# Ten of 32 weighted sums scaled on ScalarE and added on GpSimd, and three of eight stores issued one stage later

## What is computed

```python
def _L0_ffn_ref(x, router_w, router_b, expert_w, expert_b):
    xf = x.reshape(bs, h)
    S = softmax(xf @ router_w + router_b)            # 16 experts
    G, idx = top_k(S.T, bs // 16)                    # each expert takes 256 rows
    out = einsum('ekh,hd->ekd', xf[idx], expert_w) + expert_b
    return zeros.at[idx].add(G[..., None] * out)

x = x + 0.5 * _L0_ffn_ref(layernorm(x), ...)         # stage A
x = x + _L0_attn_ref(layernorm(x), ...)              # stage B: differential attention
x = x + 0.5 * _L0_ffn_ref(layernorm(x), ...)         # stage C
```

## Time and profile before

| | |
|---|---|
| time, median of 3 runs | 1705.95 us (1698.11, 1705.95, 1711.32) |
| the profiled execution's own time | 1705.67 us |
| its span, first to last instruction | 1703.3 us |
| busy: PE, DVE, ACT, POOL | 84%, 84%, 73%, 66% of the span |
| search of stage A ends (cw written) | 166.86 us from the span's start |
| weighted sums on VectorE | 166.89 to 188.18 us |
| first statistics of stage B | 190.86 us |
| first scores of attention on VectorE | 271.36 us |

### The profile page before, as it was taken

How to read it: one execution, slowest core, us unless ns; L and a number is a source line. 1 busy time by engine, 2 the same in 40 slices (tenths; PEclk the granted TensorE clock), 3 DMA queues, 4 the chain that set the end, 5 groups by cost and what they waited for, 6 DMA issues and landing times. The chain is left out here.

```text
span 1703.3 us, 46200 instructions
## 1 busy us (share of the span) xinstructions
PE 1423.8 (84%) x10988; PEld 976.8 (57%) x10988; DVE 1433.6 (84%) x5825; ACT 1251.0 (73%) x3426; POOL 1118.5 (66%) x1493
## 2 busy tenths in 40 slices
PE   3999485999899999999999999999999899998710
PEld 2644242666666666666666666666666566666400
DVE  5868635899999999999999999999999688784587
ACT  2355154889899899999898998899899677775420
POOL 4412273776788888888888888888888666664300
PEclk9999797999999999999999999999999899898855
DMA  9012514111111121211121222111121100001196
GB/s 328 1 38 56 203 36 94 31 30 41 37 50 49 49 60 49 52 48 48 48 54 48 52 54 54 50 49 49 49 60 43 39 23 18 18 18 43 50 361 241
DMA packets 166283, 116.01 MB, mean 68 GB/s; under 512 B 122577, under 2 KB 126801, under 8 KB 166226
## 3 DMA queue, kind: packets, MB, share of 16 engines
q1 hardware_dynamic: 166226, 115.33, 23.2%
HBM read 50.26 MB, written 33.55 MB: 49 GB/s over the span
## 5 line engine op out<-in xcount | busy, mean ns | idle before, releaser
L1708 ACT ACTIVATE ex<-bank,nbias 128x512 f32<-128x512 f32 (+3 forms) x1024 | 542.1, 547 | 32.7 <-DVE bank L1229 32.0
L1229 DVE TENSOR_SCALAR_CACHE_REDUCE bank<-bank,nesc 128x512 f32<-128x512 f32 (+3 forms) x1024 | 506.0, 553 | 58.2 <-PE bank L1979 57.0
L1549 POOL TENSOR_SCALAR ex<-ex,esum,gam 128x128 f32<-128x128 f32 (+3 forms) x512 | 349.4, 690 | 0.0
L2008 PE MATMUL bank<-vs,pr 128*128 (+1 forms) x2560 | 330.5, 278 | 14.6 <-DVE att L1277 12.2
L2008 PEld LDWEIGHTS bank<-vs,pr 128*128 128x128 f32 x2560 | 312.8, 195 | 51.4 <-DVE att L1277 26.5
L1725 ACT ACTIVATE pr<-bank 128x128 f32<-128x128 f32 (+3 forms) x512 | 232.7, 455 | 126.6 <-PE bank L1991 125.7
L1977 PE MATMUL bank<-ks,hall 96*128 (+2 forms) x1024 | 267.5, 307 | 30.5 <-DMA hall<-hall 18.3
L1256 DVE CUSTOM_DVE_ANT_0 df<-ex 128x128 f32<-128x128 f32 (+3 forms) x512 | 277.2, 560 | 12.7 <-issue 5.3
L1991 PE MATMUL bank<-cst,df 128*128 128x128 f32 x1280 | 237.2, 285 | 40.3 <-ACT pr L1725 37.9
L1708 ACT ACTIVATION_READ_ACCUMULATOR ex<-bank,nbias 128x1 f32 x1024 | 233.1, 228 | 0.0
L1979 PE MATMUL bank<-mask_b,ident_b 128*128 128x128 bf16 x1024 | 208.6, 223 | 0.0
(11 more groups left out here) (360 smaller groups left out, 2999.4 us busy)
## 6 DMA issues: line engine op xcount, KB each, us to landing
hall<-turned SPq DMA_DIRECT2D x336, 64.0 KB, 2.1
x_dram<-hall SPq DMA_DIRECT2D x8, 1024.0 KB, 4.9
hall<-x_dram SPq DMA_DIRECT2D x8, 1024.0 KB, 14.3
c_y<-y_dram SPq DMA_DIRECT2D x8, 1024.0 KB, 14.4
out_dram<-hall SPq DMA_DIRECT2D x8, 1024.0 KB, 4.7
hall<-in_x SPq DMA_DIRECT2D x7, 1024.0 KB, 14.3
x<-x_dram SPq DMA_DIRECT2D x28, 256.0 KB, 2.6
x_dram<-x SPq DMA_DIRECT2D x28, 256.0 KB, 2.7
```

Of the source, the lines that this page charges most:

```text
L1229: dve.tensor_scalar(part, part, nesc[:, 0:1], None, ALU.mult, ALU.min, accum_out=nbias[:, j, i, a:a + 1]).then_inc(bias_done.sem, 1)
L1549: gp.tensor_scalar(ex[j % 4][:, 1, lo:hi], ex[j % 4][:, 1, lo:hi], esum[:, j, i, 0:1], gam[:, j, i:i + 1], ALU.mult, ALU.mult).then_inc(sc ...
L1708: ac.activation(ex[j % 4][:, a, lo:hi], energy(j, i)[:, a, :], ACT.Exp, bias=nbias[:, j, i, a:a + 1], scale=-1.0, accum_out=esum[:, j, i, ...
L2008: mm = pe.matmul(bank[:, 7, t * DV:(t + 1) * DV], pr[j % 2][:, lo + k * P:lo + (k + 1) * P], val, start=(k == 0), stop=(k == t))
```

## The change

Of the 32 weighted sums, those of tiles 2, 5, 8, ... 29 (`ADDED`, ten tiles) leave VectorE, which now makes 22. For each of the ten, ScalarE scales y in place by its column of cw (`activation` with Copy) and GpSimd adds it to x1 in place. ScalarE's last two `take`s come after five and after eight of these scalings. Stores 5 to 7 (`SENT_LATE = 3`) are issued at the start of stage B's block, ahead of `load_again(0)`; they need no wait there, as all engines have passed the barrier. The other five wait for both engines' counts.

```diff
+        SENT_LATE = 3
...
+            def weights_out(self):
+                return self.decided(self.ITER - 1) + 13
...
+            y_scaled, x1_added = sem1("y_scaled"), sem1("x1_added")
+            ADDED = tuple(range(2, NT, 3))
...
-                for g in range(NT // 4):
-                    sp.wait_ge(x1_done, 4 * g + 4)
+                for g in range(NT // 4 - SENT_LATE):
+                    added = sum(u < 4 * g + 4 for u in ADDED)
+                    sp.wait_ge(x1_done, 4 * g + 4 - added)
+                    sp.wait_ge(x1_added, added)
                     sp.dma_start(x1_d[g // (TB // 4)].rearrange("(t p) e -> p t e", p=P), x1_at(4 * g, 4))\
                       .then_inc(x1_st[g], 16)
...
                 for u in range(NT):
+                    if u in ADDED:
+                        continue
                     dve.wait_ge(y_out, u + 1)
...
+                for k, u in enumerate(ADDED):
+                    gp.wait_ge(y_scaled, k + 1)
+                    gp.tensor_tensor(x1_at(u)[:, 0, :], y[:, u, :], x1_at(u)[:, 0, :], ALU.add).then_inc(x1_added, 1)
...
-                while taken[0] < NT:
+                while taken[0] < NT - 2:
                     take(taken[0])
                     taken[0] += 1
+                ac.wait_ge(choice.v, choice.weights_out())
+                for k, u in enumerate(ADDED):
+                    assert u < taken[0]
+                    ac.wait_ge(y_out, u + 1)
+                    ac.activation(y[:, u, :], y[:, u, :], ACT.Copy, scale=cw[:, u:u + 1]).then_inc(y_scaled, 1)
+                    if k in (4, 7) and taken[0] < NT:
+                        take(taken[0])
+                        taken[0] += 1
...
                 sp.sem_inc(x_in, 16 * AHEAD)
+                for g in range(NT // 4 - SENT_LATE, NT // 4):
+                    sp.dma_start(x1_d[g // (TB // 4)].rearrange("(t p) e -> p t e", p=P), x1_at(4 * g, 4))\
+                      .then_inc(x1_st[g], 16)
```

More of the change, by code:

```diff
@@ L382, in vector @@
                                        esc[:, SC_E:SC_E + 1], 0.5, ALU.mult, ALU.mult))
+                assert base[0] == self.weights_out()
             def scalar(self, ac, between=lambda i: None):
@@ L829, in _ @@
                 choice.scalar(ac, between)
-                while taken[0] < NT:
+                while taken[0] < NT - 2:
                     take(taken[0])
                     taken[0] += 1
+                ac.wait_ge(choice.v, choice.weights_out())
[6 more added lines that the diff above has]
+                        taken[0] += 1
+                assert taken[0] == NT
             @blk.tensor
```

## The result

The changed kernel took 1737.76 us, median of 4 runs (1733.4 to 1740.28), against 1702.1 us for the kernel before, 4 runs (1698.11 to 1711.32): ratio 1.0197, 95% interval 1.0168 to 1.0226. I had forecast 1710 us (1702 to 1716). It is slower by some 33 us (32.7 between the two profiled executions, 35.7 between the medians), not by 4.

A forecast was written before the change was run, and what follows sets the result against it. VectorE's run of weighted sums was taken to bound the kernel until the barrier. Exclusion between sums and additions, +4.7 us, and late stores, -0.4, gave +4.3 on 1705.67: 1710 us, range 1702 to 1716.

The forecast's parts named there:

- What bounds the kernel: Until the barrier before stage B, VectorE's run of sums is the path; the stores have about 39 us of slack.
- Part 1: VectorE's run before the barrier: ten sums leaving take 6.6 us off; 22 are left, 14.7 us.
- Part 2: Ten scalings on ScalarE after cw: cost 0, covered by its 18.83 us idle time; 6.3 us without that cover.
- Part 3: GpSimd's ten additions and VectorE's sums exclude each other, 1.79 us a pair: run 25.9 us against 21.2, +4.7 us.
- Part 4: Three stores moved behind the barrier: SP no longer arrives last, -0.4 us; the late issues and landings cost 0.
- The sum of the edited stretch: From cw to stage B's first statistics: +4.7 - 0.4 = +4.3 us.
- the last sentence of the sum: From the barrier on, stage B's prologue, stacking and attention should only be shifted.
- my rivals: At sums and barrier: no exclusion, 1698.7 us, chance 0.10; no hand-over overlap, 1713.1, 0.15; move does not matter, 1705.7, 0.07.
- Range and chances: Whole time: 1702 to 1716 us; faster by over 1% 0.01, within 1% 0.97, slower by over 1% 0.02.
- Slower by over 1%: Whole time more than 1%, or 17 us, above before; no case reached it, chance 0.02.
- What I said the profile would show: Sums and additions stretched to about 1.8 us while GpSimd adds; first statistics to first attention scores unchanged at 80.5 us.
- my signs of being wrong at the root: First statistics to first attention scores changes by over a microsecond, or the sums and additions keep their lengths.

The follow-up runs named there:

- e7: Kernel before, with ten filler memsets on VectorE and the ten sums left out, done by nobody: 1699.93 us, one run.
- e4: Changed kernel with ten filler memsets on VectorE, its 22 sums reading a PSUM bank in place of y (wrong values): 1694.52 us, ratio 0.9915.
- e1: Changed kernel plus ten tiny filler memsets on VectorE in stage A, making its list as long as before: 1706.96 us, ratio 1.0017.
- e2: Kernel before, with ten tiny memsets that start stage A's search moved from VectorE to GpSimd: 1732.39 us, ratio 1.0175.
- e9: Kernel before plus 220 or 92 filler memsets on VectorE in stage A: 1783.31 and 1778.92 us, one run each.
- e11: Kernel before plus 106 filler memsets on VectorE in stage A: 1718.4 us, one run.
- e5: Kernel before, with five tiny memsets that start stage A's search moved from VectorE to GpSimd: 1705.93 us, one run.

## Why the prediction was wrong, point by point

**What bounds the kernel** until the barrier: right. e7 shows the 6.6 us taken off the run again in full at the statistics; the stores had their slack. In the changed kernel SP still waited 33.4 us for GpSimd's low half after the last landing:

```profile
SPq L85 <- POOL att L1610: 33.4, 1, 33.4
...
SPq L1191 <- DMA x_dram<-hall: 6.8, 2, 3.7
```

**Part 1, ten sums less**: 6.6 us, as measured in e7 (24.28 - 17.65).

**Part 2, scalings at no cost**: right. GpSimd waited once for ScalarE, before its first addition. A scaling took 0.63 us:

```profile
165.62 3.17 ACT L852 ACTIVATE y<-y,cw 128x512 f32<-128x512 f32 x5 [2.11 <-DVE cw L385]
```

**Part 3, the exclusion**: the mechanism is right, in turns as forecast, and e4 shows it. The term was over-sized: a pair of addition and sum takes 1.68 us, not 1.79, so that the run is 24.76 us and not 25.9. I had taken the hand-over from the earlier trace rows, where VectorE's instruction was another one; the overlap at a hand-over is larger here, 1.27 + 0.74 - 1.68 = 0.33 us a pair.

**Part 4, late stores**: right, -0.5 for -0.4.

**The sum of the edited stretch**: +4.3 forecast, +2.9 measured. e1 gives it on the whole time: 1.0017 (1.0002 to 1.0032), +0.3 to +5.5 us of 1704.4.

**The failed step** is the last sentence of the sum: "From the barrier on, stage B's prologue, the stacking and the attention are the same instructions in the same order and should only be shifted." They are the same instructions in the same order, at other places of VectorE's instruction memory, and that costs some 28 to 30 us of the 33: VectorE fetches code again at each jump back of the first and the last attention loop. None of my rivals had it. I had priced each engine's instructions by what they do and never by where the following ones come to lie. e1 and e2 show it from both sides, e9 and e11 by forecasting which loop loses.

**Range and chances**: the range had run scatter and port exclusion in it and nothing for code that is not edited. Slower by over 1% had a chance of 0.02 and came true. That the kernel came out slower, as forecast, is mostly luck: the exclusion that I forecast makes 2.9 of the 33 us.

**What I said the profile would show**: the sums and additions stretched to the same pace, yes; the statistics to the first scores unchanged, 80.7 for 80.5, yes. My check ended at the first scores, and neither of my signs of being wrong at the root came up. The first stall ends at 351.1 us, 78 us after the first scores, at the first jump back of the first loop.

What stays open: why a stall is 4.9 us in the changed kernel and 2.0 to 2.9 in e9 and e11; and the offset of a few places between the three loops. The traces say this much on the first: of the packets of a pass two start within a stall of the changed kernel (389.8 to 394.7 us) and one within a stall of e11 (384.2 to 387.1 us):

```profile
q14 instruction: 2, 0.02, 1.2%
...
q14 instruction: 1, 0.01, 1.4%
```

## What to carry to other kernels

An edit that changes the number of instructions ahead of a hardware loop moves the loop's code, and on VectorE, the one engine measured here, that alone cost up to 4.5%; count each engine's list before and after, and look at the instruction queues' packets and at "issue" waits at the jump back before believing any explanation by the edit itself. To price an edit on the chip, run it a second time with idle fillers that put the later loops back where they were. And before moving work from VectorE to GpSimd, look at how many inputs VectorE's instructions at that time have in SBUF: with two, an addition here cost 1.0 us of the shared time to save 0.66; with one (e4) both engines ran at full speed.

## What the hardware showed that I had not expected

- A loop of 269 to 300 instructions on VectorE runs without repeated fetches at most of the places tried, and fetches 4 to 5 packets of 8,192 bytes a pass at others, at 2.0 to 5.0 us of stall a pass. The difference is a few places: five fewer cost nothing that one run shows (e5), ten fewer cost 1.75% (e2).
- The effect reaches 78 us when the main loop is hit: 92 fillers that take under 3 us together make the kernel 4.2% slower.
- TensorE runs dry in a stall of VectorE, and its granted clock then falls from 2.4 to 1.2 GHz for a while: the mean over the passes is 0.93 in the changed kernel and in e2 and 1.00 in e1 and before, which adds to the loss.
- The sums and the additions, which exclude each other and both have a queue behind them, took strict turns: ten sums and ten additions at 1.68 us a pair with no turn missed.
